# Expert rows in 24 tiles of two sizes instead of 23 of one size, with the table of tiles made on VectorE

## The reference, cut to what matters

```python
topw, topi = jax.lax.top_k(router_weights, K)          # K = 2 of E = 8 experts
topw = jax.nn.softmax(topw, axis=-1)
combine = jnp.zeros((T, E), xf.dtype).at[jnp.arange(T)[:, None], topi].add(topw)
h = jax.nn.gelu(jnp.einsum('td,edf->etf', xf, w1) + b1[:, None, :], approximate=False)
eo = jnp.einsum('etf,efd->etd', h, w2) + b2[:, None, :]
out = jnp.einsum('etd,te->td', eo, combine)
```

## Time and profile before

| what | value |
|---|---|
| median of 3 runs | 1184.55 us |
| the profiled execution | 1184.76 us, of which the span of instructions is 1183.0 us |
| granted TensorE clock, mean of the span | 0.974 of full |
| PE, weight load, DVE, ACT, POOL busy | 90, 76, 72, 65, 44% of the span |
| expert part, barrier to last matmul | 872.9 to 1149.0 us |
| after the last matmul | 34.0 us |

### The profile page before, as it was taken

One profiled execution on the slowest core, in us unless ns is written; L12 is line 12 of the kernel. 1 busy time (PEld: TensorE's weight loads), 2 busy tenths in 40 slices (PEclk: granted clock), 3 DMA queues, 4 the chain that ended last, 5 costly groups with the idle time before them and its releaser, 6 DMA issues. The chain is left out here.

```text
span 1183.0 us, 28106 instructions
## 1 busy us (share of the span) xinstructions
PE 1069.2 (90%) x9431; PEld 901.0 (76%) x9431; DVE 847.9 (72%) x2555; ACT 766.8 (65%) x1606; POOL 520.6 (44%) x737
## 2 busy tenths in 40 slices
PE   7788888889999999999989988988989999999981
PEld 7466656668888888887767766765779999999980
DVE  2777888877766566666777777665548888888866
ACT  4365576667666666656656666655539888989853
POOL 4355555422221223435666445543342444545454
PEclk9799999999999999999999999999989999999995
DMA  8566755855455444336574965551555877778735
GB/s 162 91 94 150 92 102 88 103 77 65 64 63 90 55 60 54 62 52 134 101 98 78 139 128 91 91 83 55 218 196 178 242 229 238 238 234 246 233 64 152
DMA packets 110097, 147.60 MB, mean 125 GB/s; under 512 B 22432, under 2 KB 93984, under 8 KB 104096
## 3 DMA queue, kind: packets, MB, share of 16 engines
q1 hardware_dynamic: 99760, 133.77, 54.2%
q0 software_dynamic: 8352, 10.80, 4.8%
q10 hardware_dynamic: 1872, 1.60, 1.1%
HBM read 73.54 MB, written 21.62 MB: 80 GB/s over the span
## 5 line engine op out<-in xcount | busy, mean ns | idle before, releaser
L1091 ACT ACTIVATE probs<-s 128x384 f32<-128x384 f32 (+1 forms) x512 | 264.4, 540 | 137.1 <-PE s L839 126.6
L1173 DVE TENSOR_REDUCE neg_max<-s 128x2 f32<-128x512 f32 x256 | 168.5, 688 | 65.6 <-PE s L811 58.7
L839 PE MATMUL s<-q_stack,k_stack 98*128 98x256 bf16 (+1 forms) x1024 | 174.9, 260 | 20.1 <-ACT probs L1091 18.7
L670 POOL TENSOR_SCALAR_AFFINE_SELECT probs<-probs 128x256 f32<-128x256 f32 x256 | 105.9, 422 | 166.0 <-ACT probs L1091 165.4
L1170 DVE CUSTOM_DVE_ANT_0 s<-s,mask_qk 128x256 f32<-128x256 f32 x256 | 114.0, 445 | 54.5 <-PE s L808 44.3
L839 PEld LDWEIGHTS s<-q_stack,k_stack 98*128 98x128 bf16 x1024 | 88.1, 98 | 47.6 <-ACT probs L1091 31.8
L861 PE MATMUL pv<-probs,v 128*32 128x256 f32 (+1 forms) x2048 | 110.1, 355 | 1.7 <-POOL probs L670 1.4
L1777 DVE TENSOR_TENSOR e_hidden_lo<-e_hidden,e_hidden_hi 128x512 fp32r<-128x512 f32 x92 | 78.3, 852 | 39.0 <-ACT e_hidden_hi L1716 37.8
L1607 PE MATMUL moe<-e_w_hi,e_hidden_hi 128*128 128x256 f32 x368 | 104.5, 284 | 0.5 <-DVE e_hidden_lo L1777 0.5
L1607 PE MATMUL moe<-rows_hi,e_w_hi 128*128 128x256 f32 x368 | 103.7, 282 | 1.1 <-DVE rows_lo L1773 1.1
L1607 PE MATMUL moe<-rows_hi,e_w_lo 128*128 128x256 f32 x368 | 103.2, 280 | 0.0
(11 more groups left out here) (251 smaller groups left out, 3014.7 us busy)
## 6 DMA issues: line engine op xcount, KB each, us to landing
k_stack<-k_part SPq DMA_DIRECT2D x192, 128.0 KB, 4.3
w<-in_expert_w SPq DMA_DIRECT2D x24, 1024.0 KB, 5.2
q_stack<-q_part SPq DMA_DIRECT2D x180, 128.0 KB, 6.2
w_next<-in_expert_w SPq DMA_DIRECT2D x20, 1024.0 KB, 5.1
rows<-slots_x SPq DMA_DIRECT2D x23, 256.0 KB, 2.7
slots_x<-filler SPq DMA_DIRECT2D x8, 518.0 KB
cT<-in_context SPq DMA_DIRECT2D x16, 256.0 KB, 6.3
e_b<-in_expert_b SPq DMA_DIRECT2D x23, 128.0 KB, 3.6
```

Source lines behind the costliest of these rows:

```text
L670: pool.affine_select(out=blocks, in_=blocks, compare_op=ALU.is_ge, fill=0.0, base=0, pattern=[[0, TILES], [1, P]], channel_multiplier=-1). ...
L839: last = pe.matmul(dst[:, kt * S:kt * S + S - q0], k[:, kt * P:(kt + 1) * P], q[:, q0:S], start=True, stop=True)
L1091: act.activation(probs_of(n, hd)[:, 0:width], s2[hd % 2][:, 0:width], ACT.Exp, scale=SCALE).then_inc(probs_ready, 1)
L1173: dve.tensor_reduce(neg_max[:, :, hd], src[:].rearrange("p (t s) -> p t s", t=TILES), AX_X, ALU.max, negate=True).then_inc(s1_free, 1)
```

## The change

The tiles get two sizes. `UNIT` is 128 rows; there are 39 units instead of 46 (4096 rows and at most 127 unused ones per expert). Tile 0, and the odd tiles 1 to 15, are single (one unit, 128 rows): 9 of them. The even tiles 2 to 14 and the tiles 16 to 23 are double (256 rows): 15 of them. That makes 24 tiles and 4992 rows instead of 23 and 5888. A single tile loads both matrices as a double one does; its `up` has 48 matmuls of 128 columns, its `down` 24 matmuls of 256 columns, its `turn` two transposes and not four. Its hidden values are split two quarters at a time. Two units, of experts 0 and 1, are fixed as tiles 0 and 1; every other tile is looked up.

The tables are now made in two steps: `count_units` at the end of the first part, and `fill_table` at the head of DVE's expert part. SP looks up tile 2 behind a new wait for it. The engines' loops are written out, so that tile numbers and table places are constants.

```diff
-SLOT_TILES = (TOP * B * S + E * (GROUP - 1)) // GROUP
-PAIRS = SLOT_TILES // 2
-PLACES = SLOT_TILES + 2
+UNIT = P
+UNITS = (TOP * B * S + E * (UNIT - 1)) // UNIT
+FIXED = 2
+SINGLE = E - 1
+DOUBLE = (UNITS - FIXED - SINGLE) // 2
+SLOT_TILES = FIXED + SINGLE + DOUBLE
+SIZE = [1 if n == 0 or n % 2 and n < 2 * (SINGLE + 1) else GT for n in range(SLOT_TILES)]
+PLACES = DOUBLE + SINGLE
...
-            def tiles_of_experts():
...
+            def count_units():
+                ends, key = table["ends"], table["key"]
+                doubles, singles = iota_s[:, 0:DOUBLE], iota_s[:, 0:SINGLE]
...
+                then(dve.tensor_scalar(units_i[:], counts[:], float(UNIT - 1), None, ALU.add))
+                then(dve.tensor_scalar(units_i[:], units_i[:], UNIT.bit_length() - 1, None, ALU.logical_shift_right))
...
+                dve.tensor_scalar(rests_i[:, 0], units_i[:], 1, None, ALU.logical_shift_right)
+                then(dve.tensor_scalar(rests_i[:, 1], units_i[:], 1, None, ALU.bitwise_and))
...
@@ sync
             sp.wait_ge(w1_lo_ready, QUARTERS)
-            fetch_first(2, 0)
+            sp.wait_ge(table_ready, 1)
+            e, at = expert(2), source(2)
+            fetch_first(e, 2)
             sp.wait_ge(rows_T_full, 1)
-            fetch_rows(2 * EXPERT_TILES, 0)
+            fetch_rows(at, 2)
...
+            def step(n):
+                next_e, e, at = expert(n + 1), expert(n + 2), source(n + 2)
                 sp.wait_ge(rows_T_full, n + 1)
-                fetch_rows(at, i)
+                fetch_rows(at, n + 2)
...
-            with sp.Fori(0, LOOPED) as j:
-                for i in (1, 0):
-                    n = j * 2 + 2 - i
-                    e, next_e, at = expert(n + 2), expert(n + 1), source(n + 2)
-                    step(n, i, e, at)
...
+            for n in range(1, last_tile - 1):
+                step(n)
@@ tensor
-                            last = pair_products(up_bank[q][:, m * GROUP:(m + 1) * GROUP], [w[i][:, k, f * P:(f + 1) * P] for w in (w1_hi, w1_lo)],
-                                                 [r[i][:, k, :] for r in (rows_hi, rows_lo)], k == 0, k == KC - 1)
+                            last = pair_products(up_bank[q][:, m * w:(m + 1) * w], [weights[i][:, k, f * P:(f + 1) * P] for weights in (w1_hi, w1_lo)],
+                                                 [r[i][:, k, 0:w] for r in (rows_hi, rows_lo)], k == 0, k == KC - 1)
...
-                for m in range(GT):
+                for m in range(SIZE[n]):
@@ scalar
-                    act.drain()
-                    act.activation(hidden_hi[i][:, 2 * q:2 * q + 2, :], hidden[:, 2 * q:2 * q + 2, :], ACT.Copy).then_inc(hidden_hi_ready, 1)
+                    if (q + 1) % at_once == 0:
+                        act.drain()
+                        f = slice(2 * (q + 1 - at_once), 2 * q + 2)
+                        act.activation(hidden_hi[i][:, f, 0:w], hidden[:, f, 0:w], ACT.Copy).then_inc(hidden_hi_ready, at_once)
@@ vector
+            def fill_table():
+                wide = [P, PLACES, CLASSES]
+                key = table["key"][:]
+                then(dve.tensor_tensor(past[:], table["ends"][:].rearrange("p two e -> p (two e)").unsqueeze(1).to_broadcast(wide), key.unsqueeze(2).to_broadcast(wide), ALU.is_le))
...
+                then(dve.tensor_reduce(passed[:], past[:], AX_X, ALU.add))
...
+                then(dve.tensor_tensor(past[:], past[:], table["step"][:].unsqueeze(1).to_broadcast(wide), ALU.mult))
...
+                then(dve.tensor_reduce(first[:], past[:], AX_X, ALU.add))
...
+                dve.tensor_scalar(tile_source[:], first[:], 1.0, None, ALU.add).then_inc(table_ready, 1)
...
+            fill_table()
+            rows_low(0)
```

More of the change, by code:

```diff
@@ L1287, in then @@
                 dve.drain()
-            def tiles_of_experts():
-                dve.tensor_copy(tile_expert[:, 0:E], iota_e[:])
-                dve.tensor_scalar(tile_source[:, 0:E], iota_e[:], float(EXPERT_TILES), None, ALU.mult)
-                then(dve.scalar_tensor_tensor(out=counts[:], in0=iota_e[:], scalar=-float(REGION), in1=next_slot[:], op0=ALU.mult, op1=ALU.add))
[L1294 to L1310, removed]
-                then(dve.scalar_tensor_tensor(out=source_f[:], in0=passed[:], scalar=float(EXPERT_TILES), in1=iota_s[:], op0=ALU.mult, op1=ALU.add))
-                then(dve.scalar_tensor_tensor(out=source_f[:], in0=source_f[:], scalar=1.0, in1=start[:], op0=ALU.add, op1=ALU.subtract))
-                then(dve.tensor_scalar(tile_source[:, E:], source_f[:], float(E * EXPERT_TILES), None, ALU.min))
@@ L1421, in moe_part, with nth, loads_of_weights, added_by @@
         QUARTERS = FC // 2
-        ADDED = 16 * GT
         last_tile = SLOT_TILES - 1
-        LOOPED = PAIRS - 1
+        def nth(n):
+            return n // 2 + 1
+        def loads_of_weights(n):
+            return n // 2 + n % 2
+        def added_by(n):
+            return 16 * (GT + sum(SIZE[other] for other in range(n % 2, n + 1, 2)))
+        def width(n):
+            return SIZE[n] * P
         TURNED = (2, 4)
@@ L1594, in _, with turn @@
         def _(pe):
-            def turn(n, i, nth):
-                pe.wait_ge(rows_loaded[i], 16 * nth)
+            def turn(n):
+                i, g, w = n % 2, SIZE[n], width(n)
+                pe.wait_ge(rows_loaded[i], 16 * nth(n))
                 for k in range(KC):
-                    for m in range(GT):
-                        last = pe.transpose(turn_bank[i][:, k * GROUP + m * P:k * GROUP + (m + 1) * P], rows[i][:, m, k * P:(k + 1) * P], ident[:])
+                    for m in range(g):
+                        last = pe.transpose(turn_bank[i][:, k * w + m * P:k * w + (m + 1) * P], rows[i][:, m, k * P:(k + 1) * P], ident[:])
                 last.then_inc(rows_T_full, 1)
@@ L1608, in pair_products, with up @@
                 return last
-            def up(n, i, quarters=range(QUARTERS), first=False):
+            def up(n, quarters=range(QUARTERS)):
+                i, w = n % 2, width(n)
                 if quarters[0] == 0:
@@ L1643, in _ @@
             idle(WARM_ROWS)
[L1644 removed]
+            turn(0)
             idle(WARM_HALVES)
[L1646 to L1660 removed]
+            up(0, range(0, 2))
+            turn(1)
+            up(0, range(2, QUARTERS))
+            for n in range(1, last_tile - 1):
+                up(n)
+                turn(n + 1)
+                down(n - 1)
+            up(last_tile - 1)
+            turn(last_tile)
+            down(last_tile - 2)
+            down(last_tile - 1)
+            up(last_tile)
+            down(last_tile)
             def turn_rows(u):
```

388 lines of the change are left out of this document (214 added, 174 removed).

## The result

| kernel | median us | runs | ratio to before (95% interval) |
|---|---|---|---|
| before | 1185.47 | 4 | |
| changed | 1215.10 | 4 | 1.0237 (1.0210 to 1.0264) |
| forecast | 1179.5 (1171 to 1190) | | |

The kernel before has one run more here than ahead of the prediction. The changed kernel is 2.4% slower; the forecast was 0.4% faster. The profiled execution took 1215.04 us with a span of 1213.3. The first part ended 2.35 us later than in the profile of before (SP's first load of rows at 875.24 against 872.89), and the stretch after the last matmul is 34.0 us before and 34.2 now. So the expert part itself, from that load to the last matmul, went from 276.1 us (872.89 to 1149.0) to 303.9 (875.24 to 1179.1): 27.8 us longer, where 5 less were forecast.

The account below looks back on a forecast made before the run. PE was taken as the bound at 11.65 us a step, with a weight-load chain 1 us per pair behind. Start -6.3, middle -10.5, end +11.65 sum to -5.1 from 1184.76, giving 1179.5 us, range 1171 to 1190.

Parts of the forecast that it names:

- The table and the barrier: Start of the expert part: `fill_table` takes 3.3 us, covered; the longer unit count hides under SP's wait, 0 to +0.5.
- The half-width matmul: PE, 128-column matmuls in a single's `up`: 111 ns each, set by the weight load, so 5.33 us, almost nothing saved.
- Rival four: PE: a half-width matmul costs more than a wide one's 114 ns; at 150 ns some 1191 us at worst; chance 0.05.
- The start: First tiles of the expert part: tile 2's `up` at 892.3 instead of 898.63, -6.3 us.
- A: PE step with a double's `up` and a single's `turn` and `down`: 10.4 us, of which 8.5 is PE's work.
- B: PE step with a single's `up` and a double's `turn` and `down`: 11.37 us, set by PE.
- the load chain: Second matrix split, SP's issues, first matrix landing, ACT and DVE to `rows_lo`: 21.8 us per pair, the new bound.
- a term for the landing: Within the chain of weight loads: the matrix takes 5.1 us to land, the earlier trace's median.
- PE idles about 1.9 us in each A: PE before each single's first matmul: waits about 1.9 us, the difference between 10.4 and 8.5.
- the clock: Rival: clock halves behind PE's idle, before a double's `down`; 2 us in half the pairs plus late chain, +16, 1196; chance 0.04.
- the busy share stays above 90% in the stage: The prediction's argument against the clock falling on PE in the expert part; the clock was to stay 1.00.

Follow-up runs that it names:

- the run with the loads out of the way: Changed kernel with SP fetching each tile's first matrix one step earlier; 1204.88 us, ratio 1.0178.
- the first run with transposes: Changed kernel with fourteen 128-column transposes on PE before each single tile's `up` from tile 3, loads unchanged; 1205.01 us, ratio 1.0192.
- the last run: Changed kernel with the first matrix fetched one step earlier and twelve transposes on PE ahead of a single's `up`; 1184.93 us, ratio 0.9995.

## Why the prediction was wrong

*The table and the barrier*: right. The table took 3.3 us as forecast, and SP's first load came 2.5 us after POOL's last scatter (3.1 before), so the longer count hid.

*The half-width matmul*: right. 5.41 / 48 = 113 ns, forecast 111; a single's `up` saves nothing. Rival four (over 114 ns) failed at full clock. The Trainium skill ("TensorE: Matmul & The Clock Gate", section "LDWEIGHTS (loading the stationary operand)") gives a weight load's nanoseconds as its columns over 1.2, by estimate 107 for 128 columns; the trace's 113 agrees within 6.

*The start*: short by about 1 us. Tile 2's `up` came 20.5 us after the first load of rows, forecast 19.4 (892.3 - 872.9; 0.2 of that is a slip, since 9.2 less 0.8 less 1.1 is 7.3 and not 7.1). Its weights were not late, having landed 5.4 us after their issue for the 6.9 assumed; DVE stood 3.4 us before `row_data` of tile 0, a wait on the queue ahead of `rows_lo` that the working left out.

*A and B*: right in size by luck, half right in cause. A was 10.2 to 10.8 in six of seven, 11.6 once; B at full clock 11.5. The forecast had the load chain alone behind A. In the profile that chain ended last in two of the seven, the steps of tiles 6 and 14 (10.8 and 11.6), which are the two behind a B step at full clock. The other five (10.2 to 10.5) are ACT's four quarters with `rows_hi` behind them, as long as in the run with the loads out of the way (10.2 to 10.5): the slow B step ahead of each had given the load time. Without falls the load chain sets every A, at 10.8 to 12.0 (the first run with transposes), since the loads of odd tiles then land in 5.6 to 6.7 us and not in 5.1. So the forecast's 10.4 had a term for the landing that was too small, and met the measured steps through ACT's order, which it didn't have. Only with both chains shorter A is 8.7.

*The step that failed* is the one behind it: "PE idles about 1.9 us in each A" was entered as lost time of that size and nothing else. The rival that priced the rest, the clock, had 0.04, because "the busy share stays above 90% in the stage", and 2 us in half the pairs. The share did stay above 90% (180.60 of 195.00 us from tile 2 to tile 17), and the clock fell in five of seven single tiles, for 4.8 to 6.4 us each. The mechanism was named, behind the idle of A; its chance, its price and the reason against it were wrong. The price was put on a double's `down`, but most of it lay in the half-width `up` (9.2 us for 5.4 in tile 7), in which no fall ended. The reason failed because PE's busy share was no sign of the clock here: 16.32 of 16.40 us busy at a mean of 0.69, and in the last run 20.50 of 20.50 at 0.50. The runs with 256 columns behind the same gap and with transposes in it show that at gaps of 0.7 to 1.4 us it took the idle and the half-width matmuls together.

| from the forecast to the profile, expert part | us |
|---|---|
| forecast against before | -5.1 |
| five B steps at lower clock: 84.7 - 5 x 11.48 | +27.3 |
| tile 2 later behind the shares of tile 0 | +1.1 |
| tile 2 to 3: 13.35 for 11.6, with a fall in tile 2's `up` | +1.8 |
| the other A steps (74.0 for 72.8), B at 11.48 for 11.37 | +2.0 |
| tile 17 to the end: 88.4 for 87.3 | +1.1 |
| sum; measured: 303.9 - 276.1 | 28.2; 27.8 |

The 27.3 are not all to be had back by holding the clock: in the first run with transposes, without these falls, the expert part was 22.7 us shorter, since its A steps wait longer for the loads. At 281.2 us it is still 10 above the forecast (276.1 - 5.1).

A warning stood in the earlier trace rows: in the stretch from 263.60 PE was busy 3.08 of 3.50 us at clock 0.51. A busy PE on the lower level was in view, and the busy share was used against the rival all the same.

What stays open: why the kernel with transposes but late loads varies from 1194.17 to 1215.60 us, and why a gap of 1.33 to 1.34 us ahead of 128 columns took the clock with it in three of eight single tiles and not in the other five.

## What to carry to other kernels

Idle on TensorE has two prices: its own length, and the clock it may take with it. Before an edit makes matmuls narrower, or opens a gap in front of them, ask both at once; here a gap of 0.7 to 1.4 us took no clock ahead of 256 columns in 11 cases, and some 5 us in 5 of 11 ahead of 128. Narrower matmuls saved next to nothing here (110 to 113 ns for 114 to 118, each with its weight load), so the unused columns could as well be streamed.

When work is taken off the bound, look for every chain that was hidden within the saving: of two of nearly one length, removing either leaves the other (10 us each here, 43 both). And a slow step can hide a late load in the step behind it: price a repair with the slow steps gone.

## What was not expected of the hardware

- At the lower clock the width doesn't matter to the distance. Half-width matmuls stand 0.22 us apart in the rows above (961.00, 961.22), wide ones as far, here in a `down` of the changed kernel (PE in order of time):

```profile
922.68 0.41 PE L1646 MATMUL moe<-e_w_hi,e_hidden_lo 128*128 128x256 f32 x1
922.90 0.41 PE L1646 MATMUL moe<-e_w_lo,e_hidden_hi 128*128 128x256 f32 x1
```

  At full clock they stand 0.110 to 0.113 and 0.114 to 0.118 us apart.
- A TensorE that was busy without a gap stayed on the lower level through 16 us of half-width matmuls (880.5 to 896.8 in the last run), and rose 3.4 us into wide ones. In the changed kernel it rose 1.6 to 4.1 us into them.
- The clock also falls in the first part, at other places in each execution (at 168.8, 725.2 and 810.5 us in the changed kernel's profile, at 263.6 in that of before). SP's first load of the expert part came between 871.9 and 877.9 us in the twelve profiles, which is why stretches are compared here from that load; that the falls alone move it is not shown.
